# Passages between stages of a one-core stack: split inverse deviations, first strips by VectorE, fewer products of zeros, one bank per output chunk

## The reference

```
x = x + L0(gn(x))      attention
x = x + L1(gn(x))      scan along the width, PReLU
x = x + L2(gn(x))      attention
x = x + L3(gn(x))      scan along the height, ReLU

gn(v):  (v - mean) / sqrt(var + 1e-5)   over 16 channels x 256 positions
attention(v):  e1 = relu(w1 v + b1), e2 = relu(w2 v + b2), a = relu(w3 v + b3)
               alpha * v softmax(e1' e2)' + a
scan(v), 16 strips: s[0] = v[0];  s[t] = act(W s[t-1] + b) + v[t]          (t = 1..15)
                    then back:    r[15] = s[15]; r[t] = act(W r[t+1] + b) + s[t]
```

## Time and profile before

| | us |
|---|---|
| median of 3 runs (281.57 to 281.76) | 281.69 |
| the profiled execution | 282.56 |
| its span | 280.8 |
| PE busy | 269.4 (96%) |
| DVE busy | 173.5 (62%) |
| ACT busy | 99.3 (35%) |
| POOL busy | 64.8 (23%) |

### The profile page before, as it was taken

One profiled execution on the slowest core, in us unless ns is written; L12 is line 12 of the kernel. 1 busy time (PEld: TensorE's weight loads), 2 busy tenths in 40 slices (PEclk: granted clock), 3 DMA queues, 4 the chain that ended last, 5 costly groups with the idle time before them and its releaser, 6 DMA issues.

```text
span 280.8 us, 11061 instructions
## 1 busy us (share of the span) xinstructions
PE 269.4 (96%) x4539; PEld 228.4 (81%) x4539; DVE 173.5 (62%) x634; ACT 99.3 (35%) x229; POOL 64.8 (23%) x94
## 2 busy tenths in 40 slices
PE   6999999999979999999999999999999999999996
PEld 2488888888478888888885688878786699999996
DVE  2685464555657777777777866464567455555553
ACT  2054554545643333333330337646457400000000
POOL 0109300004222222233331130000012433334432
PEclk9999999999999999999999999999999999999999
DMA  7980000000000000000000000000000000002222
GB/s 227 413 349 5 1 0 2 1 0 0 0 5 4 0 0 0 0 0 0 0 0 1 0 0 2 1 1 0 2 0 0 2 0 0 0 8 68 75 75 75
DMA packets 4479, 9.25 MB, mean 33 GB/s; under 512 B 624, under 2 KB 3056, under 8 KB 3952
## 3 DMA queue, kind: packets, MB, share of 16 engines
q1 hardware_dynamic: 4176, 8.53, 8.3%
q10 hardware_dynamic: 288, 0.52, 0.5%
HBM read 6.96 MB, written 2.10 MB: 32 GB/s over the span
## 4 chain that ended last, share of the span: by engine, by line
PE 66%; DVE 23%; ACT 4%; issue 3%; DMA 2%; POOL 1%; DVEq 0%; ACTq 0%; POOLq 0%
PE banks L377 25%; PE banks L298 19%; DVE state L717 10%; DVE sloped L712 9%; PE banks L354 6%; PE banks L310 5%; PE banks L270 4%; PE banks L317 2%; ACT xn L455 2%; PE banks L329 2%; DMA x<-in_x 2%; DVE st L543 1%; PE banks L279 1%; PE banks L345 1%; ACT rel L468 1%
## 5 line engine op out<-in xcount | busy, mean ns | idle before, releaser
L377 PE MATMUL banks<-state,wc 128*64 128x64 f32 x3840 | 126.0, 224 | 3.3 <-DVE state L717 1.5
L377 PEld LDWEIGHTS banks<-state,wc 128*64 128x64 f32 x3840 | 119.2, 138 | 10.3 <-DVE state L717 5.8
L298 PE MATMUL banks<-xn,w 128*128 128x256 f32 x256 | 60.9, 383 | 0.0
L298 PEld LDWEIGHTS banks<-xn,w 128*128 128x128 f32 x256 | 46.5, 190 | 6.5 <-issue 1.3
L695 DVE SCALAR_TENSOR_TENSOR state<-banks,negb,inb 128x64 f32<-128x64 f32 x116 | 29.3, 282 | 25.3 <-PE banks L377 23.8
L832 POOL TENSOR_TENSOR rstd<-gvar,mhalf 128x4 f32<-128x4 f32 (+1 forms) x8 | 14.6, 1827 | 123.4 <-DVE gvar L576 123.4
L712 DVE SCALAR_TENSOR_TENSOR sloped<-banks,par,share 128x64 f32<-128x64 f32 x116 | 30.1, 280 | 14.8 <-PE banks L377 14.8
L354 PE MATMUL banks<-probT,xnT 128*128 128x256 f32 x128 | 29.5, 381 | 0.8 <-ACT rel L468 0.8
L717 DVE SCALAR_TENSOR_TENSOR state<-sloped,bent,banks 128x64 f32<-128x64 f32 x112 | 28.8, 278 | 2.0
L354 PEld LDWEIGHTS banks<-probT,xnT 128*128 128x128 f32 x128 | 24.2, 190 | 4.8 <-ACT rel L468 1.6
L498 ACT COPY banks<-inb 128x256 f32 (+1 forms) x29 | 10.9, 376 | 44.4 <-DVE state L717 42.0
(11 more groups left out here) (76 smaller groups left out, 211.8 us busy)
## 6 DMA issues: line engine op xcount, KB each, us to landing
w<-in_w SPq DMA_DIRECT2D x2, 1024.0 KB, 10.7
wc<-in_wc SPq DMA_DIRECT2D x2, 1024.0 KB, 13.9
result<-xh SPq DMA_DIRECT2D x15, 128.0 KB, 1.8
x<-in_x SPq DMA_DIRECT2D x3, 512.0 KB, 9.0
x<-in_x ACTq DMA_DIRECT2D x1, 256.0 KB, 4.6
x<-in_x SPq DMA_DIRECT2D x1, 256.0 KB, 4.4
w<-in_w ACTq DMA_DIRECT2D x1, 256.0 KB, 5.0
w<-in_w SPq DMA_DIRECT2D x1, 256.0 KB, 12.2
```

The costliest lines, as they stand in the source:

```text
L298: mm = nc.tensor.matmul(bank[2 + m // 2][:, m % 2 * POS:(m % 2 + 1) * POS], w3[l][:, k, m * P:(m + 1) * P], xn_s[:, k], start=(k == 0), st ...
L377: mm = nc.tensor.matmul(bank[K * h + m][c:c + TILE, 0:COLS], wc[l][:, k, m * P + c:m * P + c + TILE], state[:, h, k], start=first and not ...
```

## The change

It has five parts, and line numbers of the new code stand in the order pieces below.

1. `rstd` of a round of 4 columns is computed as two powers of 2 columns, each with its own count on `rstd`. The readers on VectorE (first image of an attention, first state and first inputs of a scan) wait for `rstd` alone and compute (x - mean) x rstd, where they waited for `nmr` and computed x rstd + nmr. ScalarE still waits for `bmr`.
2. In a scan, strips 1 and 2 of the last image's inputs (`EARLY` = 3) are written by VectorE: four instructions over two strips and one addition of the bias. ScalarE writes strips 3 to 15. In the PReLU scan it does chunks 0 and 1, then `share` and the bank input of the first two steps, then chunks 2 and 3. Steps 0 and 1 on VectorE wait only for images 0 to 2 and for `early`.
3. Products of zeros: 13, 4, 9, 4 ahead of the means (from 9, 6, 12, 6), 2, 3, 3, 3 behind them (from 3 each), 3, 5, 6, 5 behind the variances (from 11, 11, 9, 11); all go to bank 3.
4. Output chunk 1 goes to bank 7, each chunk counts on `o_mm`, and VectorE takes them one at a time: x, then its statistics.
5. The two instructions of the first state of images 0 to 2 move from the last image of the attention into the wait behind `set_variances` and behind `variances`.

```diff
-WARM_STATS = [9, 6, 12, 6]
-WARM_MEANS = [3, 3, 3, 3]
-WARM_VARIANCES = [11, 11, 9, 11]
+WARM_STATS = [13, 4, 9, 4]
+WARM_MEANS = [2, 3, 3, 3]
+WARM_VARIANCES = [3, 5, 6, 5]
+WARM_BANK = [3, 3, 3, 3]
+EARLY = 3
...
         def o_bank(m):
-            return bank[(4, 4, 5, 6)[m]][:, (0, POS, 0, 0)[m]:(POS, 2 * POS, POS, POS)[m]]
+            return bank[(4, 7, 5, 6)[m]][:, 0:POS]
...
-                        if m:
-                            mm.then_inc(s.o_mm, 1)
+                        mm.then_inc(s.o_mm, 1)
...
             def prelu_inputs():
                 s = scan[1]
                 act.wait_ge(s_sign, 1)
-                act.wait_ge(s.inb, NC)
+                scan_inputs(1, xw, 1, (N - 1,), EARLY, range(K // 2))
+                act.wait_ge(s.inb, NC - K)
+                act.wait_ge(s.early, K + 1)
                 step_inputs(0, 1, 0)
                 step_inputs(1, 2, 1)
-                with act.Fori(0, (T - 4) // 2) as i:
+                scan_inputs(1, xw, 1, (N - 1,), EARLY, range(K // 2, K))
+                act.wait_ge(s.inb, NC)
+                with act.Fori(0, (T - 1 - EARLY) // 2) as i:
...
             def normalise_first(l):
-                dve.wait_ge(norm[l].done, 1)
                 for k in range(K):
+                    dve.wait_ge(norm[l].rstd, k * 2 // K + 1)
...
-                    nc.vector.tensor_scalar(dst, image_in(l, 0)[:, k], rstd[:, k:k + 1], nmr[:, k:k + 1],
-                                            ALU.mult, ALU.add).then_inc(att[l].xn_ready, 1)
+                    nc.vector.tensor_scalar(dst, image_in(l, 0)[:, k], gmean[:, k:k + 1], rstd[:, k:k + 1],
+                                            ALU.subtract, ALU.mult).then_inc(att[l].xn_ready, 1)
...
-                    if last:
-                        first_states(l + 1, image_rows[l])
-                    for i, ms in enumerate(((0, 1), (2,), (3,))):
-                        dve.wait_ge(s.o_mm, n * 3 + i + 1)
...
+                    for m in range(K):
+                        dve.wait_ge(s.o_mm, n * K + m + 1)
...
+            def last_norm(l, xr):
+                set_variances(l, 1)
                 dve.wait_ge(norm[l].done, 1)
                 nc.vector.tensor_tensor(strip(rest), strip(xr[:, 0]), wide(rstd), ALU.mult).then_inc(scan[l].scaled, 1)
+                variances(l, 1)
                 dve.wait_ge(scan[l].scaled, 1)
                 nc.vector.tensor_tensor(strip(state[:, 0]), strip(rest), wide(nmr), ALU.add)
...
+                place = slice((N - 1) * T, COLS)
+                for ks in (range(K // 2), range(K // 2, K)):
+                    dve.wait_ge(norm[l].rstd, 1 + ks[-1] * 2 // K + 1)
+                    for k in ks:
+                        c = (N - 1) * K + k
+                        mm = nc.vector.tensor_scalar(state[:, 0, k, place], xr[:, 0, k, place],
+                                                     gmean[:, c:c + 1], rstd[:, c:c + 1], ALU.subtract, ALU.mult)
+                        mm.then_inc(s.state[k], 1)
+                    for k in ks:
+                        c = (N - 1) * K + k
+                        nc.vector.tensor_scalar(inb[:, 1:EARLY, k, place], xr[:, 1:EARLY, k, place],
+                                                gmean[:, c:c + 1], rstd[:, c:c + 1], ALU.subtract, ALU.mult)\
+                            .then_inc(s.early, 1)
+                dve.wait_ge(s.early, K)
+                nc.vector.tensor_tensor(inb[:, 1:EARLY, :, place], inb[:, 1:EARLY, :, place],
+                                        cb.unsqueeze(1).unsqueeze(3).to_broadcast([P, EARLY - 1, K, T]), ALU.add)\
+                    .then_inc(s.early, 1)
...
-                dve.wait_ge(s.inb, NC)
-                step(0, 1, 0)
...
+                dve.wait_ge(s.inb, NC - K)
+                dve.wait_ge(s.early, K + 1)
+                for q in range(EARLY - 1):
+                    step(q, q + 1, q % 2)
+                dve.wait_ge(s.inb, NC)
...
             def inverse_std(l):
...
+                    width = K // 2 if c1 - c0 == K else c1 - c0
                     pool.wait_ge(s.gvar, r + 1)
-                    nc.gpsimd.tensor_tensor(rstd[:, c0:c1], gvar[:, c0:c1], mhalf[:, c0:c1], ALU.pow)\
-                        .then_inc(s.rstd, 1)
+                    for c in range(c0, c1, width):
+                        nc.gpsimd.tensor_tensor(rstd[:, c:c + width], gvar[:, c:c + width], mhalf[:, c:c + width],
+                                                ALU.pow).then_inc(s.rstd, 1)
+                        done += 1
```

More of the change, by code:

```diff
@@ L103, in __init__ @@
         self.inb = sem(f"inputs_ready{l}")
+        self.early = sem(f"first_inputs_ready{l}")
         self.y = [sem(f"products_done{l}_{u}") for u in units]
@@ L266, in _, with keep_warm @@
         def _(pe):
-            def keep_warm(count, b=7):
+            def keep_warm(count, b):
                 for _ in range(count):
@@ L671, in scan_layer @@
                     chain[0] += 1
-                dve.wait_ge(norm[l].done, 2)
-                for k in range(K):
-                    c = (N - 1) * K + k
-                    mm = nc.vector.tensor_scalar(state[:, 0, k, (N - 1) * T:], xr[:, 0, k, (N - 1) * T:],
-                                                 rstd[:, c:c + 1], nmr[:, c:c + 1], ALU.mult, ALU.add)
-                    mm.then_inc(s.state[k], 1)
+                place = slice((N - 1) * T, COLS)
[6 more added lines that the diff above has]
+                        mm.then_inc(s.state[k], 1)
+                    for k in ks:
+                        c = (N - 1) * K + k
[6 more added lines that the diff above has]
+                    .then_inc(s.early, 1)
                 def product(k, h):
@@ L746, in step @@
                         relu_step(q, t, h)
+                dve.wait_ge(s.inb, NC - K)
+                dve.wait_ge(s.early, K + 1)
+                for q in range(EARLY - 1):
+                    step(q, q + 1, q % 2)
                 dve.wait_ge(s.inb, NC)
-                step(0, 1, 0)
-                with dve.Fori(0, (T - 2) // 2) as i:
+                with dve.Fori(0, (T - 1 - EARLY) // 2) as i:
                     for h in range(2):
-                        step(i * 2 + 1 + h, i * 2 + 2 + h, 1 - h)
+                        step(i * 2 + EARLY - 1 + h, i * 2 + EARLY + h, h)
+                step(T - 2, T - 1, 0)
                 dve.wait_ge(s.taken, T - 1)
@@ L802, in _ @@
             attention(0, signal[:, 0:1])
-            set_variances(1, 1)
-            variances(1, 1)
-            scan_layer(1, xw)
+            last_norm(1, xw)
+            scan_layer(1, xw, signb[:])
             dve.wait_ge(scan[1].taken, 2 * T - 2)
@@ L809, in _ @@
             attention(2, signal[:, 1:2])
-            set_variances(3, 1)
-            variances(3, 1)
-            scan_layer(3, xh)
+            last_norm(3, xh)
+            scan_layer(3, xh, par[:, CB_3:CB_3 + K])
         @block.gpsimd
```

55 lines of the change are left out of this document (25 added, 30 removed).

## The result

| | before | after |
|---|---|---|
| median, us | 281.69 (281.15 to 281.79, 5 runs) | 279.63 (278.83 to 280.53, 5 runs) |
| ratio | | 0.9934, 95% interval 0.9914 to 0.9954 |
| the profiled execution, its span | 282.56, 280.8 | 279.35, 277.5 |
| DVE busy | 173.5 (62%) | 177.2 (64%) |
| products of zeros | 25.4 us, 87 | 15.9 us, 57 |

The account below looks back on a forecast made before the run. Bound: one dependence that changes engines, TensorE holding 66% and VectorE 23%. Terms 0.87 + 1.40 + 0.20 + 1.38 - 0.46 = 3.4 us took the median from 281.69 to 278.3; own range 277.8 to 278.9, 8-in-10 range 277.2 to 279.8.

Parts of the forecast that it names:

- Passage 0, 0.87: Start of attention 0: earlier `xn` and statistics bring the maximum of the scores and second variances 0.87 us earlier.
- the 0.63 of slack: Passage 0: the maximum of the scores waited 0.63 us for TensorE; counted with 0.27 from image loads as 0.9 earlier.
- Passage 1, first step, 1.00: Start of the PReLU scan: half powers and early strips let VectorE start step 0 1.00 us earlier.
- Passage 3, first step, 0.98: Start of the ReLU scan: TensorE is through step 0 at 222.77, not 223.68, its bound; gain 0.98 us.
- Statistics, 0.40: Passage 1, last image of the attention: first output starts earlier, statistics end at 72.38, not 72.78; gain 0.40 us.
- passage 2, 0.20: Start of attention 2: `xn` waited just 0.17 for `nmr`, so the gain is 0.2 us, not 0.8.
- Middle images, -0.46: Attention 2, images 1 and 2: four single outputs end later than before, TensorE stalls 0.23 us each, -0.46 together.
- The power's cost is mostly fixed: Rival: each half power costs 1.01 us, shrinking the first-step gains in passages 1 and 3; 279.8 us, chance 0.12.
- cost double: Same rival's paragraph: instructions on strips of 32 columns costing double would give the same time, 279.8 us.
- The loads do not hold passage 0: Rival: passage 0 then gives 3.0 us and the sum is 5.5; 276.2 us, chance 0.04.
- The slower rival: TensorE's clock falls in passages with fewer zeros, 2.3 us each; 280.6 with one, 282.9 with two; chance 0.06.

Follow-up runs that it names:

- a_again: The kernel after, unchanged, run again with its own trace: 279.44 us median, ratio 0.9931.
- c_pool: The kernel after, with GpSimd's first addition in each scan (L870) waiting until VectorE has finished the early inputs: 278.65 us, ratio 0.9897.
- b_again: The kernel before, unchanged, run again with its own trace: 281.54 us median, ratio 1.0.
- c_pair: The kernel after, with VectorE taking outputs of all images but the last in the old order (a pair, then two singles): 279.56 us, ratio 0.994.
- e_loads: The kernel after, with the last quarter of the first attention's w3 weights loaded behind the images instead of ahead: 279.27 us, ratio 0.9911.
- a_fill: The kernel after, with more products of zeros ahead of the means and behind the variances: 280.11 us, ratio 0.9946.
- c_noearly: The kernel after without part 2: ScalarE writes all 15 strips of the last image, VectorE none; half powers stay: 281.57 us, ratio 0.9984.

## Why the prediction was wrong, step by step

The sum was 1.33 too high. The missing parts are 0.44 in passage 0, 0.66 in the first step of passage 1 and 0.57 in that of passage 3; the middle images and last statistics gave back 0.31.

**Passage 0, 0.87: mis-sized, 0.43.** The working counted "the 0.63 of slack" at the maximum as gain. That slack existed in the earlier trace rows only because the zeros ran at half pace in that execution. At full pace VectorE's own string (`xn`, 12 statistics, constants, copy, maximum) holds the passage in the kernel before as well, without a wait. What is left is the earlier start of `xn`, 0.60, less 0.16, since `xn` takes 1.54 beside the second power and 1.38 behind it. And the last step of the sum could not mend it: "it stood 0.87 above the median, so the median goes from 281.69 to 278.3" took the excess for a constant outside the kernel's stages, while it sat in passage 0, part of it in the very wait that the sum counted as gain. Measured against its own execution the forecast was close, 282.56 less 279.35 is 3.2 for 3.4, but by luck: there passage 0 gave 1.72 (20.22 to 18.50) for 0.87, and the rest 1.5 for 2.5.

**Passage 1, first step, 1.00: failed, 0.34.** Of the missing 0.66, from the rows of `a_again` and from 3.38 forecast between the power's start and `rest` against 4.03 measured: the two half powers took 1.41 for 1.20 (0.21); ScalarE's two inputs 1.01 for 0.92 (0.09); `share` waited 0.18 for L691, which the forecast had done 2.75 behind the power's start (77.5) and which was done at 3.22; the rest, 0.17, is in the steps from the power to ScalarE and from `share` to VectorE. The wait for L691 is the interference that `c_pool` takes away.

**Passage 3, first step, 0.98: failed, 0.41.** The sentence that failed is "VectorE's step 0 must be started by 222.4, which the early inputs allow". It had no sum behind it. 222.4 is 2.71 behind the power's start; VectorE was there at 3.32 (216.86 to 220.18). TensorE waited for it, so the bound that I had worked out, through the chunks of the first state, was the shorter of two. With L870 held back VectorE is there at 2.90 (216.60 to 219.50) and the gap is gone; behind `gvar`, 3.14 against 3.97 in `b_again`: 0.83 of the 0.98.

**Statistics, 0.40, and passage 2, 0.20: right.** 0.42 and 0.21. One bank for each chunk and the moved first state did what they say, under the cover that was named.

**Middle images, -0.46: mis-sized.** About -0.2. The wait was there and as long as forecast; a weight load's wait is not a wait of the products. The rule of the Trainium skill that a semaphore after each instruction costs nothing ("VectorE: DVE Perf Modes", "The DRAIN you can't avoid") would make the two orders equally long, and they are not: four alternations went from the first output's start at 182.45 to the last one's end at 185.23, 2.78, and the pair with two singles took 2.52 in `b_again` (183.65 to 186.17) and the same in `c_pair`, where all else is as after (182.62 to 185.14). In both orders every instruction counts on a semaphore; what differs is a wait on the instruction just ahead: two outputs without it start 0.34 apart, and the statistics that wait for their output start 0.44 to 0.46 after it. Only TensorE's cover made it nearly free.

**The rivals.** "The power's cost is mostly fixed" gave 279.8, near the measured time, for half of the right reason and so partly by luck. The powers cost 0.70, between my 0.60 and its 1.01; the same paragraph named instructions on strips of 32 columns that "cost double", and one of the four did, for a cause not named there. "The loads do not hold passage 0" was right for most traces, but its gain of 3.0 did not follow, since VectorE's string holds it. The slower rival exists as a mechanism, a fall of TensorE's clock behind a passage, in some executions, at 0.8 to 0.9 and not 2.3 each. The kernel before has executions at .994 too: among those run beside `a_again` they are no slower than the others (281.6 both), and among those beside `e_loads` they are the quicker ones (median 281.5; four of the five at 1.0 took 282.5 to 282.7). So a mean of .994 is nothing new and no sign of a costly fall by itself. The prediction's list of idle stretches left out the pause ahead of the PReLU scan's second step, which grew from 1.48 to 1.94; the counts above, 29 of 53 against 2 of 29, speak for it as the cause of the fall near 80, but that the longer pause makes it more frequent than before is not shown, since no trace of the kernel before has a fall. Why it does not come always stays open.

## What to carry to other kernels

Run the kernel before more than once ahead of reading gains off a stage: if the profiled execution is above the median, find the stage in which the excess sits before it is carried as a constant. Where a step waits for two engines, work out both to a tenth of a microsecond, also the one that "allows" it. Small VectorE instructions that are moved onto the path should not run beside a GpSimd instruction that nobody waits for; here one wait on GpSimd brought 0.8 us on top of the 2.1 of the change.

## What the hardware showed that I had not expected

- An instruction of VectorE over 32 columns in two strips, with two per-partition operands, took 0.70 to 0.72 us beside a GpSimd `tensor_tensor` of 256 columns, and 0.30 with that one held back; GpSimd's next took 0.87 beside VectorE and 0.73 later. In passage 0 the four of `xn` took 1.54 beside a power and 1.38 without it, and GpSimd's `nmr` 0.36 beside `xn` and 0.20 otherwise.
- A power on GpSimd took 0.69 to 0.74 us for 2 columns (0.83 beside `xn`), 1.01 to 1.05 for 4, 2.71 for 12.
- The pace of TensorE in the first ten microseconds differs between executions of one kernel (11 products in 4.65 or in 2.53) while the granted clock reads 1.00 in both. The slow pace at 7 us was seen in two of three traces with 9 products of zeros at the start, and in none of eleven with 13.
- The granted clock fell to 0.50, the 1.2 GHz level, for about 3 us behind a pause of 1.94 us in one execution and stayed at 1.00 behind the same pause in others. The fall cost 0.8 to 0.9 us near 80 us (`a_fill`, `c_noearly`).
